# Two attention layers, a routed and a spline feed-forward on one core: causal row maxima taken with the mask added in the vector engine's own operation

## Chip, cores and metric

One NeuronCore of a Trainium2 chip runs the whole program. The metric is device time in microseconds (us), the median over several executions. Engines: TensorE (PE), VectorE (DVE), ScalarE (ACT), GpSimd (POOL), and SyncE (SP), which here only starts transfers (DMAs).

## The reference, cut to what matters

The input is x of shape 32 x 256 x 128 (32 sequences of 256 tokens, 128 features). Four blocks follow each other, each with a residual and a layer norm: attention with LoRA, a routed feed-forward of 8 experts, causal attention with rotary embedding, and a spline feed-forward. The change concerns the third:

```
qkv = x @ w_qkv                                  # 16 heads of 8 features
q, k = q * cos + rotate_half(q) * sin, k * cos + rotate_half(k) * sin
att = einsum('bhtd,bhsd->bhts', q, k) * scale
att = where(causal, att, finfo.min)
att = softmax(att, axis=-1)
y = einsum('bhts,bhsd->bhtd', att, v) ... @ w_proj
```

## The kernel before, in words

`attention` builds both attention layers: `attn0` (not causal) and `attn1` (causal, with rotary embedding). It is a software pipeline over the 32 sequences (`pipeline`, line 79): in each step every engine works on up to five sequences at different ages ("lag" 0 to 4), and each engine's program is written out by hand as 16 slots n = 0 to 15. The table `AT` says at which slot each small operation stands. Semaphores order the engines; a wait stops everything behind it on its engine.

A step of `attn1` does the following.

- Lag 0: PE transposes x (slot 0) and projects q and k (slot 1, L479); ACT copies them out of PSUM; POOL turns them (L257 to L261) and splits them into three bf16 parts (L267 to L277). SP stores the parts in a scratch in DRAM (L204, L206) and reads them back as the stacks `q_st` and `k_st` in six DMAs (L223). The six wait for the stores and, because they write the stack of three sequences ago, for that sequence's last column scores, which PE makes in slot 15 of the same step (`cols_ready`).
- Lag 2, the row scores, which serve only to find each query's maximum. `score_rows(st, n)` makes one unit per slot: unit u covers two heads and the query block t = u % 2, with (t + 1) * 128 keys per head, in one of three PSUM banks. Before it writes a bank it waits until DVE has taken the maximum of unit u - 3 (`max_kept`). In the causal layer it first writes the mask with one matmul (L531, 128 x 256: the identity times `mask_qk`, for both heads at once, over the diagonal blocks), and the two heads' products (L535) are added to it. `row_max` on DVE (L353) then reduces both heads in one instruction to two negated maxima in `negmax`. `split_max` (slot 9 for units 0 to 7, slot 15 for units 8 to 15) splits eight heads' maxima in two bf16 parts (L364, L366). PE transposes them (L471; slot 11 of this step, slot 1 of the next), ACT copies them, and SP places them as two more rows under q (L211, L195).
- Lag 3, the column scores: `score_cols(st, n)`, one head per slot, with the maximum already subtracted through those two rows and its own mask matmul (L553, L557); ACT takes the exponential (L297). Slot 0 waits for the first eight heads' maxima to land, slot 8 for the others (L195's DMA). `sum_values` (L574) multiplies by v in groups of four heads.
- Lag 4: transposing the output, dividing (DVE, L388 and L392, slot 3, after PE's L491 in slot 4), projection, residual, layer norm. v is copied by DVE at slot 5 (L381), the residual at slot 12 (L405, L409), the variance at slot 14 (L415, L418).

In each slot PE issues, in this order, the column scores, the row scores, and then whatever the table puts there; it has one queue. SP's queue in a step is: load of the next x (L186), L195, the two stores, L211, the six stack loads. DVE's slot begins with `row_max`.

`apart(eng, mem)` only adds one to a semaphore that nobody waits for; it keeps two waits from being merged. `mask_qk` is made once, before the first layer, by POOL in `prepare`. Masked places hold -1e30.

Of the kernel before, what the change touches and what calls it, by code (L numbers as in the profile page):

```python
# [9 lines left out]
BF16 = mybir.dt.bfloat16  # L10
I32 = mybir.dt.int32
ALU = mybir.AluOpType
ACT = mybir.ActivationFunctionType
AX_X = mybir.AxisListType.X

P = 128
B, N, C = 32, 256, 128
# [6 lines left out]
MASKED = -1e30  # L24
# [45 lines left out]
def apart(eng, mem):  # L70

    eng.sem_inc(mem["apart"], 1)


def wait(eng, sem, value):

    if not isinstance(value, int) or value > 0:
        eng.wait_ge(sem, value)
# [16 lines left out]
def attention(nc, name, mem, causal, x_dram, lora, rope):  # L95
# [7 lines left out]
    ident, ident_h, mask_qk, mask_kq = (mem[k] for k in ("ident", "ident_h", "mask_qk", "mask_kq"))  # L103
    scale = float(D) ** -0.5
# [3 lines left out]
    with ExitStack() as ctx:  # L108
        def sb(label, shape, dt=F32):
            return ctx.enter_context(nc.sbuf_tensor(f"{name}_{label}", shape, dt))  # L110

        def sem(label):
            return nc.alloc_semaphore(name=f"{name}_{label}")
# [8 lines left out]
        q_st = sb("q_st", [P, SLOTS, H, N], BF16)  # L122
        k_st = sb("k_st", [P, SLOTS, H, N], BF16)
        negmax = sb("negmax", [P, TB, H])
        mparts = sb("mparts", [P, 2, TB, MROWS, NH], BF16)
        mT_sb = sb("mT_sb", [MROWS * NH, 2, N], BF16)
        v_sb = sb("v_sb", [P, SLOTS, TB, H * 32])
# [12 lines left out]
        row_ps = ctx.enter_context(nc.psum_tensor(f"{name}_row_ps", [P, 3, 512], F32))  # L140
# [17 lines left out]
        xT_kept, qk_kept, v_kept, max_kept, mhi_kept, mparts_kept, mT_kept, probs_kept, oT_kept = (  # L158
            sem(x) for x in ("xT_kept", "qk_kept", "v_kept", "max_kept", "mhi_kept", "mparts_kept", "mT_kept",
                             "probs_kept", "oT_kept"))  # L160
# [13 lines left out]
        UNITS, ROW_BANKS = NH * TB, 3  # L174

        def row_bank(st, u):
            return (UNITS * st.off + u) % ROW_BANKS
# [166 lines left out]
        def _(dve):  # L344
            def row_max(st, u):

                p, t = u // TB, u % TB
                if u % NH == 0:

                    wait(dve, mparts_kept, st.seq(2, 2, u // NH - 1))  # L350
                dve.wait_ge(rows_ready, st.seq(2, UNITS, u + 1))
                keys = (t + 1) * P if causal else N
                nc.vector.tensor_reduce(  # L353
                    negmax[:, t, 2 * p:2 * p + 2],
                    row_ps[:, row_bank(st, u), 0:2 * keys].rearrange("p (a k) -> p a k", a=2),
                    AX_X, ALU.max, negate=True).then_inc(max_kept, 1)

            def split_max(st, g):

# [89 lines left out]
        def _(pe):  # L449
# [68 lines left out]
            def score_rows(st, u):  # L518

                sl = st.slot(2)  # L520
                p, t = u // TB, u % TB
                if u == 0:
                    pe.wait_ge(q_stacked[sl], st.turn(2, 16 * STACKS))
                    pe.wait_ge(k_stacked[sl], st.turn(2, 16 * STACKS))

                wait(pe, max_kept, st.seq(2, UNITS, u + 1 - ROW_BANKS))
                bank = row_ps[:, row_bank(st, u), :]
                keys = (t + 1) * P if causal else N
                if causal:
                    seen = bank[:, 0:2 * keys].rearrange("p (a k) -> p a k", a=2)  # L530
                    nc.tensor.matmul(seen[:, :, keys - P:keys], ident_h[:, :], mask_qk[:, :, :],  # L531
                                     start=True, stop=False, skip_group_check=True)
                for a in range(2):
                    h = 2 * p + a
                    last = nc.tensor.matmul(bank[:, a * keys:(a + 1) * keys],  # L535
                                            q_st[0:KROWS, sl, h, t * P:(t + 1) * P], k_st[0:KROWS, sl, h, 0:keys],
                                            start=not causal, stop=True, skip_group_check=causal)
                last.then_inc(rows_ready, 1)

            def score_cols(st, n):  # L540
# [1064 lines left out]
def prepare(nc, mem, w):  # L1605

    with ExitStack() as ctx:
# [3 lines left out]
        def sem(label):  # L1611
            return nc.alloc_semaphore(name=f"prep_{label}")
# [17 lines left out]
        loaded, consts, zeroed, masked = sem("loaded"), sem("consts"), sem("zeroed"), sem("masked")  # L1630
# [28 lines left out]
        @block.gpsimd  # L1659
        def _(pool):  # L1660
            for t in (mem["ident"], mem["ident_h"], mem["mask_qk"], mem["mask_kq"]):
                nc.gpsimd.memset(t[:], 0.0).then_inc(zeroed, 1)
            nc.gpsimd.memset(diagonal[:, :], 1.0).then_inc(zeroed, 1)
            nc.gpsimd.memset(mem["sigs"][:, :], 0.0).then_inc(zeroed, 1)
            nc.gpsimd.memset(mem["cw2"][:, :], 0.0).then_inc(zeroed, 1)
            nc.gpsimd.memset(mem["minus_half"][:, :], -0.5).then_inc(consts, 1)
            pool.wait_ge(zeroed, 7)
            for t in (mem["ident"], mem["ident_h"]):
                nc.gpsimd.affine_select(out=t[:, :], in_=t[:, :], compare_op=ALU.not_equal, fill=1.0, base=0,
                                        pattern=[[-1, P]], channel_multiplier=1).then_inc(consts, 1)  # L1670

            nc.gpsimd.affine_select(out=mem["mask_qk"][:], in_=mem["mask_qk"][:], compare_op=ALU.is_ge, fill=MASKED,
                                    base=0, pattern=[[0, 2], [-1, P]], channel_multiplier=1).then_inc(consts, 1)

            nc.gpsimd.affine_select(out=mem["mask_kq"][:], in_=mem["mask_kq"][:], compare_op=ALU.is_ge, fill=MASKED,
                                    base=0, pattern=[[0, 2], [1, P]], channel_multiplier=-1).then_inc(consts, 1)
            nc.gpsimd.affine_select(out=diagonal[:, :], in_=diagonal[:, :], compare_op=ALU.is_ge, fill=0.0,
                                    base=0, pattern=[[-D, H], [0, D]], channel_multiplier=1).then_inc(masked, 1)
            pool.wait_ge(masked, 1)
            nc.gpsimd.affine_select(out=diagonal[:, :], in_=diagonal[:, :], compare_op=ALU.is_ge, fill=0.0,  # L1680
                                    base=D - 1, pattern=[[D, H], [0, D]], channel_multiplier=-1).then_inc(consts, 1)
# [68 lines left out]
def build(nc, w, out):  # L1750
    with ExitStack() as ctx:
        def sb(label, shape, dt=F32):
            return ctx.enter_context(nc.sbuf_tensor(label, shape, dt))

        mem = {"x_all": sb("x_all", [P, TILES, C]), "x_mid": sb("x_mid", [P, TILES, C]),
               "ident": sb("ident", [P, P]), "ident_h": sb("ident_h", [P, P], BF16),
               "mask_qk": sb("mask_qk", [P, 2, P], BF16), "mask_kq": sb("mask_kq", [P, 2, P], BF16),
               "cos": sb("cos", [P, N]), "sin": sb("sin", [P, N]),
               "minus_half": sb("minus_half", [P, TILES])}
        for n in range(2):  # L1760
# [60 lines left out]
```

## Time and profile before

| what | us |
|---|---|
| median of 3 runs | 1542.13 |
| lowest and highest run | 1540.18, 1552.94 |
| the profiled execution, its own time | 1533.47 |
| its span in the profile | 1531.7 |

How to read it: the span begins with the first and ends with the last instruction that the profiler recorded. Busy time is the time in which an engine executes something; the matmuls' ends are modelled, so a busy PE is not PE at its peak. "PEld" is the loading of weights, which runs beside matmuls. "PEclk" is the granted clock of TensorE as a share of 2.4 GHz. Layer `attn0` runs from about 90 to 600 us of the span, `attn1` from about 700 to 1270 us.

### The profile page before, as it was taken

The numbers are of one execution on the slowest core, as the hardware profiler recorded it, in microseconds if no ns is written. First come the engines' busy times: TensorE is split into PE (matmuls) and PEld (weight loads), VectorE is DVE, ScalarE is ACT, GpSimd is POOL, SyncE is SP. The second block draws the span as 40 slices with busy tenths as digits, with TensorE's granted clock in tenths as the row PEclk, the third lists the DMA queues.
The fourth block names the chain that finished last, engine by engine and source line by source line (L and its number), as shares of the span: only waits on it lengthen the run. The fifth ranks groups of instructions, "written<-read, shape, count | busy, mean of one in ns | idle before, by whom it ended". The sixth has DMA issues, their size and how long they took to land. (4 is left out here: it accounts for less than half of the span.)

```text
span 1531.7 us, 36081 instructions
## 1 busy us (share of the span) xinstructions
PE 1142.7 (75%) x11411; PEld 786.7 (51%) x11411; DVE 1102.7 (72%) x2949; ACT 845.0 (55%) x1844; POOL 552.9 (36%) x572
## 2 busy tenths in 40 slices
PE   2699998999999987415999999999999984402220
PEld 1355655655565654203677767777777752202220
DVE  1477888888888886723677677767777757798996
ACT  1265666666666665442666666666666653302555
POOL 5222332223222311354444454445445305002555
PEclk9998999999999999756999999999999997755555
DMA  5644544445444540305444444454445302000011
GB/s 139 155 103 98 117 110 111 97 114 112 113 97 113 113 94 2 118 17 135 98 109 113 115 101 108 114 113 99 111 113 114 94 2 76 35 0 0 29 34 48
DMA packets 115921, 137.26 MB, mean 90 GB/s; under 512 B 12112, under 2 KB 101520, under 8 KB 106640
## 3 DMA queue, kind: packets, MB, share of 16 engines
q1 hardware_dynamic: 112704, 132.25, 36.2%
q10 hardware_dynamic: 3152, 4.20, 1.0%
q8 instruction: 34, 0.56, 0.2%
q14 instruction: 31, 0.25, 0.1%
HBM read 85.03 MB, written 37.75 MB: 80 GB/s over the span
## 5 line engine op out<-in xcount | busy, mean ns | idle before, releaser
L353 DVE TENSOR_REDUCE attn_negmax<-attn_row_ps 128x2 f32<-128x512 f32 (+1 forms) x1024 | 609.7, 618 | 283.0 <-PE attn_row_ps L535 273.7
L297 ACT ACTIVATE attn_probs<-attn_col_ps 128x512 f32<-128x512 f32 (+1 forms) x1024 | 542.5, 547 | 299.3 <-PE attn_col_ps L557 282.2
L557 PE MATMUL attn_col_ps<-attn_q_st,attn_k_st 74*128 74x256 bf16 (+1 forms) x2048 | 373.2, 264 | 36.7 <-DMA attn_q_st<-attn_mT_sb 34.6
L535 PE MATMUL attn_row_ps<-attn_k_st,attn_q_st 72*128 72x256 bf16 (+1 forms) x2048 | 375.3, 266 | 16.1 <-DMA attn_k_st<-attn_scratch 15.2
L574 PE MATMUL attn_out_ps<-attn_probs,attn_v_sb 128*32 128x256 f32 (+1 forms) x4096 | 255.1, 368 | 1.3 <-ACT attn_probs L297 1.3
L557 PEld LDWEIGHTS attn_col_ps<-attn_q_st,attn_k_st 74*128 74x128 bf16 x2048 | 180.6, 99 | 131.8 <-ACT attn_probs L297 41.0
L535 PEld LDWEIGHTS attn_row_ps<-attn_k_st,attn_q_st 72*128 72x128 bf16 x2048 | 204.4, 100 | 44.3 <-issue 16.7
L282 POOL TENSOR_TENSOR attn_rstd<-attn_var,minus_half 128x2 f32<-128x2 f32 x64 | 45.4, 710 | 459.7 <-DVE attn_var L418 459.7
L531 PE MATMUL attn_row_ps<-mask_qk,ident_h 128*128 128x256 bf16 x512 | 141.9, 277 | 23.5 <-DMA attn_k_st<-attn_scratch 23.5
L553 PE MATMUL attn_col_ps<-mask_kq,ident_h 128*128 128x256 bf16 x512 | 142.0, 277 | 23.3 <-DMA attn_q_st<-attn_mT_sb 22.1
L574 PEld LDWEIGHTS attn_out_ps<-attn_probs,attn_v_sb 128*32 128x32 f32 x4096 | 108.9, 111 | 90.0 <-issue 25.0
L257 POOL TENSOR_TENSOR attn_q_half<-attn_q_half,sin 128x512 f32<-128x512 f32 x32 | 40.7, 1272 | 146.4 <-ACT attn_qk L324 146.2
L1524 POOL TENSOR_TENSOR ffn_rstd<-ffn_var,minus_half 128x8 f32<-128x8 f32 x19 | 31.9, 1679 | 167.3 <-DVE ffn_var L1546 167.3
L479 PE MATMUL attn_in_ps<-attn_xT,wqk 128*128 128x256 f32 x256 | 80.6, 442 | 1.8 <-ACT attn_xT L303 1.8
L553 PEld LDWEIGHTS attn_col_ps<-mask_kq,ident_h 128*128 128x128 bf16 x512 | 49.9, 97 | 61.7 <-DMA attn_q_st<-attn_mT_sb 25.1
L267 POOL TENSOR_SCALAR attn_parts<-attn_qk 128x512 bf16<-128x512 f32 x64 | 39.5, 618 | 113.6 <-ACT attn_qk L321 102.1
L1468 PE MATMUL ffn_r_ps<-ffn_table_hm,ffn_ohT 128*128 128x193 bf16 x64 | 21.0, 361 | 75.0 <-ACT ffn_ohT L1480 75.0
L277 POOL TENSOR_TENSOR attn_parts<-attn_rest,attn_parts 128x512 bf16<-128x512 f32 x64 | 74.3, 1162 | 5.4
L270 POOL TENSOR_TENSOR attn_rest<-attn_qk,attn_parts 128x512 f32<-128x512 f32 x64 | 74.0, 1156 | 5.4
L531 PEld LDWEIGHTS attn_row_ps<-mask_qk,ident_h 128*128 128x128 bf16 x512 | 49.6, 97 | 33.0 <-issue 24.2
L1457 PE MATMUL ffn_o_ps<-ident_h,ffn_onehot 128*128 128x128 bf16 x64 | 10.1, 313 | 73.4 <-PEq L1172 73.4
L1487 ACT ACTIVATE ffn_z<-ffn_y,ffn_shift,ffn_rstd 128x128 f32<-128x128 f32 x64 | 26.3, 482 | 55.5 <-DVE ffn_shift L1551 55.5
(229 smaller groups left out, 1694.5 us busy)
## 6 DMA issues: line engine op xcount, KB each, us to landing
attn_q_st<-attn_scratch SPq DMA_DIRECT2D x192, 192.0 KB
attn_k_st<-attn_scratch SPq DMA_DIRECT2D x192, 192.0 KB
attn_scratch<-attn_parts SPq DMA_DIRECT2D x64, 384.0 KB, 2.8
attn_scratch<-attn_parts SPq DMA_DIRECT2D x64, 128.0 KB, 2.8
attn_x_in<-in_L_attn_x_dram SPq DMA_DIRECT2D x32, 128.0 KB, 7.0
moe_xs<-x_all SPq DMA_DIRECT2D x8, 512.0 KB, 3.1
attn_x_in<-x_mid SPq DMA_DIRECT2D x32, 128.0 KB, 7.0
ffn_xs<-x_mid SPq DMA_DIRECT2D x16, 256.0 KB, 2.3
```

The source lines that it names most:

```text
L257: nc.gpsimd.tensor_tensor(q_half[:, :, :], q_half[:, :, :], sin, ALU.mult).then_inc(sin_done, 1)
L270: nc.gpsimd.tensor_tensor(rest[:, :, :], qk[:, :, :], parts[:, :, 0, :], ALU.subtract)\
L277: nc.gpsimd.tensor_tensor(parts[:, :, 2, :], rest[:, :, :], parts[:, :, 1, :], ALU.subtract)\
L282: nc.gpsimd.tensor_tensor(rstd[:, :], var[:, :], mem["minus_half"][:, 0:TB], ALU.pow)\
L297: nc.scalar.activation(probs[:, u % 2, j, 0:W], col_ps[:, n % 2, 0:W], ACT.Exp, scale=scale).then_inc(probs_kept, 1)
L353: nc.vector.tensor_reduce(negmax[:, t, 2 * p:2 * p + 2], row_ps[:, row_bank(st, u), 0:2 * keys].rearrange("p (a k) -> p a k", a=2), AX_X, ...
L479: last = nc.tensor.matmul(in_ps[:, s * N:(s + 1) * N], wqk[:, s, :], xT[:, st.slot(0), :], start=True, stop=True)
L531: nc.tensor.matmul(seen[:, :, keys - P:keys], ident_h[:, :], mask_qk[:, :, :], start=True, stop=False, skip_group_check=True)
L535: last = nc.tensor.matmul(bank[:, a * keys:(a + 1) * keys], q_st[0:KROWS, sl, h, t * P:(t + 1) * P], k_st[0:KROWS, sl, h, 0:keys], start=n ...
L553: nc.tensor.matmul(seen[:, :, 0:P], ident_h[:, :], mask_kq[:, :, :], start=True, stop=False, skip_group_check=True)
L557: last = nc.tensor.matmul(bank[:, t * N:(t + 1) * N - first], k_st[0:rows, sl, h, t * P:(t + 1) * P], q_st[0:rows, sl, h, first:N], start= ...
L574: last = nc.tensor.matmul(out_ps[32 * j:32 * j + 32, g * N + first:(g + 1) * N], v_sb[:, st.slot(lag), t, 32 * h:32 * h + 32], probs[:, u ...
```

## The change

For the causal layer the mask matmul under the row scores is left out, so that the two head products start their own accumulation. On DVE the one reduction over two heads becomes two `tensor_tensor_reduce` operations, one per head. Each reads the head's scores from PSUM and the mask from SBUF (fp32, 256 columns: zeros over the first 128 keys, the triangle over the last 128; a unit with 128 keys reads the last 128), adds them, multiplies by -1, writes the sum as bf16 to a buffer `unread` that nobody reads, and gives the minimum as the negated maximum. `unread` has two halves, so a unit waits until the unit two before it has finished. The first layer keeps its reduction.

```diff
+        unread = sb("unread", [P, 2, 2, N], BF16) if causal else None
...
                 dve.wait_ge(rows_ready, st.seq(2, UNITS, u + 1))
-                keys = (t + 1) * P if causal else N
-                nc.vector.tensor_reduce(
-                    negmax[:, t, 2 * p:2 * p + 2],
-                    row_ps[:, row_bank(st, u), 0:2 * keys].rearrange("p (a k) -> p a k", a=2),
-                    AX_X, ALU.max, negate=True).then_inc(max_kept, 1)
+                if not causal:
+                    nc.vector.tensor_reduce(
...
+                    return
+                apart(dve, mem)
+                wait(dve, max_kept, st.seq(2, UNITS, u - 1))
+                apart(dve, mem)
+                keys = (t + 1) * P
+                for a in range(2):
+                    last = nc.vector.tensor_tensor_reduce(
+                        out=unread[:, u % 2, a, 0:keys], in0=row_ps[:, row_bank(st, u), a * keys:(a + 1) * keys],
+                        in1=mask_qk[:, N - keys:N], scale=-1.0, scalar=3e38, op0=ALU.add, op1=ALU.min,
+                        accum_out=negmax[:, t, 2 * p + a:2 * p + a + 1])
+                last.then_inc(max_kept, 1)
...
                 keys = (t + 1) * P if causal else N
-                if causal:
-                    seen = bank[:, 0:2 * keys].rearrange("p (a k) -> p a k", a=2)
-                    nc.tensor.matmul(seen[:, :, keys - P:keys], ident_h[:, :], mask_qk[:, :, :],
-                                     start=True, stop=False, skip_group_check=True)
                 for a in range(2):
                     h = 2 * p + a
                     last = nc.tensor.matmul(bank[:, a * keys:(a + 1) * keys],
                                             q_st[0:KROWS, sl, h, t * P:(t + 1) * P], k_st[0:KROWS, sl, h, 0:keys],
-                                            start=not causal, stop=True, skip_group_check=causal)
+                                            start=True, stop=True)
...
-            nc.gpsimd.affine_select(out=mem["mask_qk"][:], in_=mem["mask_qk"][:], compare_op=ALU.is_ge, fill=MASKED,
-                                    base=0, pattern=[[0, 2], [-1, P]], channel_multiplier=1).then_inc(consts, 1)
+            nc.gpsimd.affine_select(out=mem["mask_qk"][:, P:N], in_=mem["mask_qk"][:, P:N], compare_op=ALU.is_ge,
+                                    fill=MASKED, base=0, pattern=[[-1, P]], channel_multiplier=1).then_inc(consts, 1)
...
-               "mask_qk": sb("mask_qk", [P, 2, P], BF16), "mask_kq": sb("mask_kq", [P, 2, P], BF16),
+               "mask_qk": sb("mask_qk", [P, N]), "mask_kq": sb("mask_kq", [P, 2, P], BF16),
```

## Rows read from the trace of the kernel before

**Rows 1.** The page, busy time of each engine over the whole span
```profile
PE 1142.7 (75%) x11411; PEld 786.7 (51%) x11411; DVE 1102.7 (72%) x2949; ACT 845.0 (55%) x1844; POOL 552.9 (36%) x572
```
**Rows 2.** Windows (length, busy time per engine, PEclk, DMA): causal layer; two steps of the first
```profile
751.50:1270.00 518.50, 487.89 (x5505) 361.89 (x5503) 367.18 (x998) 324.97 (x739) 225.18 (x235) 0.99 0.43 101
388.20:404.40 16.20, 15.11 (x154) 9.98 (x152) 14.03 (x34) 11.17 (x24) 4.96 (x6) 1.00 0.49 114
404.40:422.30 17.90, 16.33 (x152) 10.40 (x151) 13.88 (x34) 11.23 (x25) 4.95 (x6) 0.91 0.45 103
```
**Rows 3.** Timeline (start us, duration us), ACT's copy L338, which comes once per step
```profile
852.82 0.36 ACT L338 COPY attn_mT_sb<-attn_in_ps 16x256 bf16<-16x256 bf16 x1
1175.47 0.36 ACT L338 COPY attn_mT_sb<-attn_in_ps 16x256 bf16<-16x256 bf16 x1
...
388.22 0.34 ACT L338 COPY attn_mT_sb<-attn_in_ps 16x256 bf16<-16x256 bf16 x1
404.43 0.34 ACT L338 COPY attn_mT_sb<-attn_in_ps 16x256 bf16<-16x256 bf16 x1
422.29 0.34 ACT L338 COPY attn_mT_sb<-attn_in_ps 16x256 bf16<-16x256 bf16 x1
```
**Rows 4.** Timeline of PE in one step of the causal layer
```profile
1036.02 0.28 PE L553 MATMUL attn_col_ps<-mask_kq,ident_h 128*128 128x256 bf16 x1 [0.71 <-DMA attn_q_st<-attn_mT_sb]
...
1043.01 0.27 PE L531 MATMUL attn_row_ps<-mask_qk,ident_h 128*128 128x256 bf16 x1
1043.12 0.38 PE L535 MATMUL attn_row_ps<-attn_k_st,attn_q_st 72*128 72x256 bf16 x2
...
1044.80 0.27 PE L471 MATMUL attn_fin_ps<-ident_h,attn_mparts 128*16 128x128 bf16 x2
```
**Rows 5.** Timeline of SP's queue in the same step
```profile
1043.20 0.32 SPq L223 DMA_DIRECT2D attn_q_st<-attn_scratch  x1
...
1046.41 0.63 SPq L195 DMA_DIRECT2D attn_q_st<-attn_mT_sb  x1
```
**Rows 6.** Waits of SP's queue, 860 to 1160 us (us in total, times, longest)
```profile
SPq L72 <- DMA attn_scratch<-attn_parts: 25.2, 18, 1.5
SPq L223 <- PE attn_col_ps L557: 4.8, 11, 0.9
```
**Rows 7.** Waits, 751.5 to 1270 us (us in total, times, longest)
```profile
DVE attn_negmax L353 <- PE attn_row_ps L535: 91.6, 159, 1.3
...
PEld attn_in_ps L501 <- ACT attn_qk L324: 6.6, 27, 0.3
```
**Rows 8.** Groups by shape, 760 to 1240 us (busy us, mean ns | idle before)
```profile
L353 DVE TENSOR_REDUCE attn_negmax<-attn_row_ps 128x2 f32<-128x512 f32 x228 | 156.4, 686 | 60.0 <-PE attn_row_ps L535 57.4
L353 DVE TENSOR_REDUCE attn_negmax<-attn_row_ps 128x2 f32<-128x256 f32 x228 | 95.4, 418 | 35.2 <-PE attn_row_ps L535 31.3
...
L392 DVE TENSOR_TENSOR attn_o_sb<-attn_fin_ps,attn_rden 128x128 f32<-128x128 f32 x58 | 14.1, 285 | 1.0
L405 DVE TENSOR_TENSOR attn_y_sb<-attn_fin_ps,x_mid 128x256 f32<-128x256 f32 x28 | 11.9, 424 | 5.0 <-PE attn_fin_ps L514 4.7
L415 DVE BATCH_NORM_AGGREGATE attn_mv<-attn_stats 128x2 f32<-128x6 f32 x56 | 6.6, 159 | 0.0
```
**Rows 9.** Timeline of DVE in one step of the causal layer
```profile
1032.73 0.36 DVE L388 RECIPROCAL attn_rden<-attn_fin_ps 128x32 f32<-128x32 f32 x1 [0.90 <-PE attn_fin_ps L491]
1033.12 0.49 DVE L392 TENSOR_TENSOR attn_o_sb<-attn_fin_ps,attn_rden 128x128 f32<-128x128 f32 x2
...
1042.83 0.23 DVE L415 BATCH_NORM_AGGREGATE attn_mv<-attn_stats 128x2 f32<-128x6 f32 x2
...
1044.47 0.17 DVE L366 TENSOR_TENSOR attn_mparts<-attn_negmax,attn_mparts 128x16 bf16<-128x16 f32 x1
...
1049.77 0.36 DVE L388 RECIPROCAL attn_rden<-attn_fin_ps 128x32 f32<-128x32 f32 x1 [0.91 <-PE attn_fin_ps L491]
```
**Rows 10.** Windows: DVE's stretch in that step, all engines, then L353 alone
```profile
1032.73:1044.64 11.91, 11.20 (x136) 8.36 (x134) 10.09 (x28) 6.71 (x15) 6.43 (x7) 1.00 0.33 84
...
1032.73:1044.64 11.91, 6.46 (x12) 1.00 0.33 84
```
**Rows 11.** Line L405, 860 to 1160 us: DVE's sequencer computing a wait's value (ns, min/median/max)
```profile
L405 DVEq FUSED_REGOPS  x18: 57/65/81, 870.9 to 1159.5; - x18
```

More of the change, by code:

```diff
@@ L351, in row_max @@
                 dve.wait_ge(rows_ready, st.seq(2, UNITS, u + 1))
-                keys = (t + 1) * P if causal else N
-                nc.vector.tensor_reduce(
-                    negmax[:, t, 2 * p:2 * p + 2],
-                    row_ps[:, row_bank(st, u), 0:2 * keys].rearrange("p (a k) -> p a k", a=2),
-                    AX_X, ALU.max, negate=True).then_inc(max_kept, 1)
+                if not causal:
+                    nc.vector.tensor_reduce(
+                        negmax[:, t, 2 * p:2 * p + 2],
+                        row_ps[:, row_bank(st, u), :].rearrange("p (a k) -> p a k", a=2),
+                        AX_X, ALU.max, negate=True).then_inc(max_kept, 1)
+                    return
[9 more added lines that the diff above has]
+                last.then_inc(max_kept, 1)
             def split_max(st, g):
```

## The prediction

> **What bounds the kernel now.** I read the page's busy line first: PE 75% and DVE 72% of the span, neither alone the bound [rows 1]. The windows view then isolates the causal layer, the only one whose steps the change touches: in 518.5 us PE is busy 487.9 us (94%), DVE 367.2 us (71%), at a granted clock of 0.99 [rows 2]. So TensorE looks like the bound and VectorE as if it had room. The step view corrects this. Nineteen steps lie between the two marks of ACT's copy, (1175.47 - 852.82) / 19 = 16.98 us each [rows 3]. In one of them PE stands still for 0.71 us at slot 8, waiting for the second half of the maxima to land from DMA [rows 4]. A full engine would not wait, so I followed that wait back through SP's timeline: the small DMA L195 is issued at 1046.41, behind the six stack loads that start at 1043.20 [rows 5], and the stack loads are released by PE's last column scores (slot 15; its row scores follow at 1043.12 [rows 4]) or by the stores before them. Both come nearly together: SP waited 25.2 us in 18 steps for the stores, and after that 4.8 us for PE [rows 6], 0.27 us a step.
>
> That gives three closed chains, and the longest sets the step:
> - Chain A: PE slot 8 (1036.02) to the stack loads (1043.20), 7.18 us, then the DMAs until the next slot 8, 16.98 - 7.18 = 9.8 us. Its length is the step itself.
> - Chain B: the same, but through q and k, ACT, POOL and the stores; it runs over two steps and is at most 0.27 us behind.
> - Chain C: DVE's second split ends (1044.47 + 0.17 = 1044.64 [rows 9]), PE transposes it at 1044.80 [rows 4], PE works through slots 1 to 4, DVE starts L388 at 1049.77 [rows 9], and then does twelve units and its other work until the next second split ends. Now it has slack: in the stretch from L388 (1032.73) to 1044.64 DVE is busy 10.09 of 11.91 us [rows 10]. Its length is 0.16 + 4.97 + 10.1 + about 0.3 of gaps between dependent instructions (of the 1.8 us idle the timeline puts most on PE; 0.3 is my estimate for the rest) = 15.5 us, 1.5 under the step.
>
> **The change, part by part.** *PE.* It loses 16 mask matmuls a step. One takes 1043.12 - 1043.01 = 0.11 us of PE's time [rows 4] (their 0.27 us are mostly pipeline), 1.8 us a step; over 32 steps that is 57 us of TensorE work gone. But chain A holds only the seven between slot 8 and slot 15's column scores: 7 x 0.115 = 0.8 us, so A becomes 16.2 us. Chain B sees the saving once in two steps: (2 x 17.0 - 0.27 - 0.92 - 0.2) / 2 = 16.3 us, and 16.4 with a later split. In chain C two of the three masks lie in front of PE's projection of v, which waits for ACT anyway (27 times, up to 0.3 us [rows 7]): only one counts, 4.97 becomes 4.85. *If nothing else changed*, the step would be 16.4 us, 0.6 less.
>
> *DVE.* The reduction over 512 elements takes 686 ns and over 256 elements 418 ns [rows 8]; twelve of them keep DVE busy 6.46 us, 0.54 a unit [rows 10]. In their place come two operations per unit of 256 or of 128 elements, each with PSUM and SBUF inputs. The trace has both shapes as plain additions: L405 (256) 424 ns and L392 (128) 285 ns [rows 8], so the slope is 139 / 128 = 1.09 ns per element and the rest some 145 ns. Back to back less counts: two L392 take 0.49 us together [rows 9], so the second starts 0.205 us after the first, which is 0.133 for its elements at the reductions' slope ((686 - 418) / 256 = 1.05 ns) and 0.07 fixed. Two heads then cost 2 x (0.267 + 0.07) = 0.68 us at 256 and 2 x (0.134 + 0.07) = 0.41 us at 128, mean 0.54: no more than today's 0.54.
>
> What no row shows is a DVE operation that gives a stream and a reduced value both. Bound from below: nothing, 0.54 a unit. Below nothing is excluded, since the same elements pass at the same slope. Bound from above: each head runs to its full end (424 or 285 ns) and then a small instruction with its full 159 ns (L415 [rows 8]) writes the value: (2 x 0.583 + 2 x 0.444) / 2 = 1.03 us a unit. I take a small instruction that is pipelined like the others: two L415 take 0.23 us [rows 9], 0.07 more than one. That is 0.14 a unit, 0.68 us in all. I take it because the reduced value can only be known after the last element, and L415 is the nearest row for a result of so few elements.
>
> The Trainium skill, "VectorE: DVE Perf Modes", section "Two Vector instructions with no wait between them", says that an operation that also writes out its accumulator is two instructions, the main one and an accumulator read. No row here shows one; by that rule the unit would be at the 0.68 and not at the 0.54, and it speaks against the change.
>
> Chain C then: 0.16 + 4.85 + other DVE work 10.09 - 6.46 = 3.63 + 12 x 0.68 = 8.2 + 0.3 = 17.1 us. This is now the longest chain, by 0.7 us over B: the idle time of DVE (91.6 us of waits for row scores [rows 7]) is used up, and PE waits for the second split in slot 1. PE's waits in slot 1 and DVE's three-bank lead do not help, since the split needs all eight pairs.
>
> *The added wait and markers.* The wait is for the unit two before, which has finished when the one before runs; behind it stand this unit's operations and all later DVE work. Value 0 as long as the sequencer runs ahead. Computing a wait's value takes 65 ns (57 to 81) of DVE's sequencer [rows 11]; if that and two markers were exposed, it is up to 3 x 0.065 = 0.2 us a unit. I take 0, with that as the upper end. *One-time parts* (the mask made once, fp32 in place of bf16; no DMA is added or moved): 0, before the first layer and behind its loads. The first layer is unchanged. The stack loads keep their place in SP's queue, and when C rules they start later.
>
> *The clock.* The first layer has no mask matmuls, and its steps show what may follow: one of 16.2 us at granted clock 1.00 is followed by one of 17.9 us at 0.91 [rows 2, 3]; at two levels (2.4 and 1.2 GHz) that is some 18% of the step at the lower one. The steps are 404.43 - 388.22 = 16.21 and 422.29 - 404.43 = 17.86 us, so a fall costs up to 1.65 us, and they come in about one step of three, 0.55 us a step. The causal layer, fuller, is at 0.99. After the change PE has 1.8 us less work and slightly longer steps, like the first layer. Since PE is no longer in the longest chain for most of the step, I take half, 0.27 us.
>
> The page "TensorE: Matmul & The Clock Gate" of the Trainium skill, section "Part 1: The HAM clock gate (the "warmup" mystery)", says that the slow clock is the default and activity releases it; by it, taking matmuls out can bring the slow clock back, as the first layer's row of 0.91 suggests.
>
> **Sum.** 17.1 + 0.27 - 16.98 = 0.39 us a step, 31 full steps: +12 us. The profiled execution took 1533.5 us, so 1545.5 us on its basis. The median of the runs, 1542.1 us, lies 8.6 us above that execution; I add the difference to the median: 1554 us. A change under 1% (15.4 us) can't be told from none here.
>
> **Rivals.**
> - R1, the reduced value comes free. Unit 0.54 us, chain C 15.5 us, the step is 16.4 from chain B: -0.58 x 31 = -18 us, 1524; with falls of the clock as above -10 us, 1532. For it: the plain additions' rows. Against: nothing shows two results at the price of one.
> - R2, the value is read only after the operation has drained. Unit up to 1.03, chain C 0.16 + 4.85 + 3.63 + 12.4 + 0.3 = 21.3 us: +4.3 x 31 = +134 us, 1676. It decides from a unit above 0.66 us, where C passes today's 16.98. For it: dependent instructions on DVE do show their full latency (L366 starts 0.2 us after the cast before it). Half of it (0.85) gives C 19.1 and +67 us, 1609.
> - R3, the sequencer is exposed (0.2 us a unit over the forecast): unit 0.88, chain C 19.5, +2.5 x 31 = +78 us at full price, 1620, and 1595 at two thirds. For it: a unit now has a second wait, two markers and two dispatches. Against: where DVE is behind, it has a unit's time to do them.
> - R4, the clock falls in every step, 1.4 to 1.6 us each, with cheap maxima: 16.4 + 1.5 = 17.9, +28 us, 1570. Against: in the first layer it falls in one of three.
>
> **Chances.** Forecast 0.42, R1 0.20, R2 0.13, R3 0.15, R4 0.10. Within the forecast's own spread (unit 0.62 to 0.75, clock 0 to 0.5 us) somewhat under half lies above +15.4 us. Faster by over 1%: half of R1 and a little of the forecast, 0.13. Within 1%: the rest of R1 and over half of the forecast, 0.37. Slower: 0.50. The range leaves out R1's last part and R2's upper half: 1524 to 1609.
>
> **What would show it.** Right: DVE's waits for row scores in the causal layer fall from 91.6 us to under 30; the two operations of a 256-key unit span some 0.8 us; PE waits for `attn_mparts` at slot 1 in most steps; the wait at slot 8 for L195 stays or shrinks; PE busy falls by about 50 us; steps of 17.1 to 17.6 us; PEclk of the layer 0.95 to 0.98. Wrong: if DVE still waits often for row scores and steps are under 16.6 us, the value came free (R1). If a head's operation and its end take over 0.5 us at 256, it is R2; if the operations are short but stand apart by 0.1 us or more with nothing released between them, R3; if the clock is under 0.93 with cheap operations, R4.

## The result and the profile after

The changed kernel takes 1578.5 us (median of 4 runs, 1572.1 to 1582.6) against 1541.2 us before: a ratio of 1.022, 95% interval 1.016 to 1.029. It is slower by 37 us. The profiled execution took 1580.4 us. The chip shows a faster and a slower state at the same kernel: ratios here compare executions in the faster one, times are medians of all.

The page's busy line and the windows view of the causal layer (columns as in [rows 2]) for the changed kernel:

```profile
PE 1121.6 (71%) x10899; PEld 751.5 (48%) x10899; DVE 1142.5 (72%) x4485; ACT 844.4 (53%) x1844; POOL 553.4 (35%) x572
```
```profile
751.50:1270.00 518.50, 437.73 (x4637) 309.59 (x4639) 372.55 (x2239) 301.16 (x688) 217.66 (x217) 0.93 0.43 99
```

TensorE lost 512 matmuls, as written, but only 21 us of busy time in the whole span, where the prediction had 57: its granted clock in this layer went from 0.99 [rows 2] to 0.93, and what is left runs longer. VectorE's busy time in the window, 372.6 us against 367.2 [rows 2], can't be compared as it stands, because fewer steps fit into the window now. In the whole span it is 40 us more (1142.5 against 1102.7 [rows 1]), and the row maxima alone, in a window of their own, before and then after, are:

```profile
860.00:1150.00 290.00, 146.58 (x274) 1.00 0.47 110
```
```profile
860.00:1150.00 290.00, 149.38 (x968) 0.93 0.43 100
```

That is 146.58 / 274 = 0.53 us a unit before and, with four instructions to a unit, 149.38 / 242 = 0.62 us after: 0.08 more, 1.3 us a step. The marks of ACT's copy, one per step (start, duration; L339 answers to L338 [rows 3]), show where the time is:

```profile
878.16 0.36 ACT L339 COPY attn_mT_sb<-attn_in_ps 16x256 bf16<-16x256 bf16 x1
...
894.53 0.36 ACT L339 COPY attn_mT_sb<-attn_in_ps 16x256 bf16<-16x256 bf16 x1
...
911.91 0.36 ACT L339 COPY attn_mT_sb<-attn_in_ps 16x256 bf16<-16x256 bf16 x1
...
937.29 0.36 ACT L339 COPY attn_mT_sb<-attn_in_ps 16x256 bf16<-16x256 bf16 x1
```

The steps are 16.4, 17.4 and 25.4 us, and so it goes on: one step in three takes 20 to 25 us. The others take 16.3 to 18.7 us, the shortest as long as the prediction had it for cheap maxima. The waits view of the same layer (us in total, times, longest) names the place:

```profile
DVE attn_unread L364 <- issue: 60.3, 50, 8.4
DVE attn_unread L364 <- PE attn_row_ps L543: 49.7, 77, 2.1
...
PEld attn_row_ps L543 <- DVE attn_negmax L364: 35.1, 9, 6.8
PE attn_row_ps L543 <- DVE attn_negmax L364: 33.0, 7, 6.6
```

"issue" is time in which the engine waited for nothing that the profile shows. VectorE stands still for 60.3 us without a releaser, up to 8.4 us at once, and TensorE then waits for it up to 6.6 us; before, this wait was 0.2 us, once. VectorE's timeline at one of these places:

```profile
804.35 0.60 DVE L435 TENSOR_SCALAR x_mid<-attn_y_sb,attn_mv,attn_rstd 128x128 f32 x2
813.38 0.29 DVE L364 CUSTOM_DVE_ANT_0 attn_unread<-attn_row_ps,mask_qk 128x128 bf16<-128x128 f32 x1 [8.44 <-issue]
```

L435 is the last operation of slot 15, and the next is slot 0 of the next step. The loop of `pipeline` covers three steps and makes eight turns, so it jumps back seven times, after a slot 15. Seven stalls (they end at 813.4, 868.6, 925.7, 984.7, 1039.7, 1096.0 and 1151.5 us) come in this place, 55 to 59 us apart, once per turn, 46 us together. An eighth, of 4.2 us, ends at 1232.6 us, in the steps that are written out behind the loop. The view of DMA queues, window 820 to 1190 us (packets, MB, share of the 16 engines; queue q14 is the one that grows here), of the kernel before and then of the changed one:

```profile
q8 instruction: 2, 0.03, 0.0%
q14 instruction: 1, 0.01, 0.0%
```
```profile
q14 instruction: 32, 0.26, 0.3%
```

Before, no engine needed more than stray packets of code in the middle of the loop. Now 32 packets of 8 KB are fetched, about five per turn. Counted in the built programs, VectorE's loop body in the causal layer has 432 instructions; before it had 190. That is the theory tested below, F: the body no longer stays in the engine's instruction memory, and each jump back waits for code. (TensorE's body in the same layer had 540 instructions before and has 492 now, and before the change hardly a packet in the middle of the loop went with it: the length that matters is not the same for both engines.)

The packets can be set beside the stalls one by one. The stall that ends at 868.60 us begins at 862.49. Between 861 and 865 us no instruction packet starts; the queues from 865 to 867 us are:

```profile
q1 hardware_dynamic: 90, 0.32, 75.6%
q14 instruction: 1, 0.01, 2.0%
```

In all 21 stalls at a jump, of this kernel and of experiments 2 and 4, the packet records have one instruction packet inside, and VectorE goes on 2.1 to 2.4 us after it ends. What differs is when it starts: 1.1 to 5.7 us after VectorE has stopped. In 20 of them the burst of the six stack loads had begun before the stall and 12 to 14 packets of data were on their way at once. In the one where the burst began 0.6 us after the stall, the packet started after 1.1 us, and this stall is the shortest, 3.8 us. So most of a long stall looks like a code packet that waits among the loads; no run moved the loads to test it.

The new operations themselves are cheap. Groups by shape, 760 to 1270 us, and VectorE's timeline inside a full stretch:

```profile
L364 DVE CUSTOM_DVE_ANT_0 attn_unread<-attn_row_ps,mask_qk 128x256 bf16<-128x256 f32 x437 | 167.5, 421 | 39.2 <-PE attn_row_ps L543 31.8 <-DVE attn_negmax L364 2.6 <-issue 2.4
...
L364 DVE CUSTOM_DVE_ANT_0 attn_unread<-attn_row_ps,mask_qk 128x128 bf16<-128x128 f32 x436 | 108.7, 287 | 76.8 <-issue 57.9 <-PE attn_row_ps L543 16.4 <-DVE attn_negmax L364 1.7
...
L364 DVE DVE_READ_ACCUMULATOR2_ANT attn_negmax<- 128x1 f32 x872 | 72.3, 83 | 0.0
```
```profile
1061.14 0.42 DVE L364 CUSTOM_DVE_ANT_0 attn_unread<-attn_row_ps,mask_qk 128x256 bf16<-128x256 f32 x1
1061.49 0.08 DVE L364 DVE_READ_ACCUMULATOR2_ANT attn_negmax<- 128x1 f32 x1
1061.49 0.42 DVE L364 CUSTOM_DVE_ANT_0 attn_unread<-attn_row_ps,mask_qk 128x256 bf16<-128x256 f32 x1
1061.83 0.08 DVE L364 DVE_READ_ACCUMULATOR2_ANT attn_negmax<- 128x1 f32 x1
1061.83 0.49 DVE L393 COPY attn_v_sb<-attn_in_ps 128x128 f32<-128x128 f32 x2
```

421 and 287 ns are the plain additions' 424 and 285 [rows 8]. The accumulator read is there as an instruction of its own, of 83 ns, but the next operation starts together with it: from one head to the next it is 0.34 us, the prediction's 0.267 + 0.07 without anything for the read.

### The profile page after: what moved, and what is told of

Its sections match the earlier page's. It is cut to its first block and busy times, and to the rows that moved or that the text cites. A ratio compares the mean times of both kernels' runs of the same rounds, so it can differ in the third digit from the quotient of the medians.

```text
span 1578.7 us, 37619 instructions
## 1 busy us (share of the span) xinstructions
PE 1121.6 (71%) x10899; PEld 751.5 (48%) x10899; DVE 1142.5 (72%) x4485; ACT 844.4 (53%) x1844; POOL 553.4 (35%) x572
## 5 line engine op out<-in xcount | busy, mean ns | idle before, releaser
L364 DVE CUSTOM_DVE_ANT_0 attn_unread<-attn_row_ps,mask_qk 128x128 bf16<-128x128 f32 (+1 forms) x1024 | 313.3, 354 | 178.1 <-PE attn_row_ps L543 108.8
L543 PE MATMUL attn_row_ps<-attn_k_st,attn_q_st 72*128 72x256 bf16 (+1 forms) x2048 | 382.2, 270 | 73.4 <-DMA attn_k_st<-attn_scratch 38.4
L354 DVE TENSOR_REDUCE attn_negmax<-attn_row_ps 128x2 f32<-128x512 f32 x512 | 335.2, 684 | 122.2 <-PE attn_row_ps L543 120.0
L565 PE MATMUL attn_col_ps<-attn_q_st,attn_k_st 74*128 74x256 bf16 (+1 forms) x2048 | 380.1, 268 | 37.9 <-DMA attn_q_st<-attn_mT_sb 35.7
L582 PE MATMUL attn_out_ps<-attn_probs,attn_v_sb 128*32 128x256 f32 (+1 forms) x4096 | 258.6, 372 | 1.3 <-ACT attn_probs L298 1.3
L565 PEld LDWEIGHTS attn_col_ps<-attn_q_st,attn_k_st 74*128 74x128 bf16 x2048 | 184.4, 101 | 136.9 <-ACT attn_probs L298 41.2
L543 PEld LDWEIGHTS attn_row_ps<-attn_k_st,attn_q_st 72*128 72x128 bf16 x2048 | 184.7, 101 | 109.1 <-issue 40.8
L561 PE MATMUL attn_col_ps<-mask_kq,ident_h 128*128 128x256 bf16 x512 | 148.3, 290 | 38.3 <-DMA attn_q_st<-attn_mT_sb 36.7
L364 DVE DVE_READ_ACCUMULATOR2_ANT attn_negmax<- 128x1 f32 x1024 | 85.0, 83 | 0.0
```

What stands on the lines that cost most here:

```text
L354: nc.vector.tensor_reduce(negmax[:, t, 2 * p:2 * p + 2], row_ps[:, row_bank(st, u), :].rearrange("p (a k) -> p a k", a=2), AX_X, ALU.max, ...
L364: last = nc.vector.tensor_tensor_reduce(out=unread[:, u % 2, a, 0:keys], in0=row_ps[:, row_bank(st, u), a * keys:(a + 1) * keys], in1=mask ...
L543: last = nc.tensor.matmul(bank[:, a * keys:(a + 1) * keys], q_st[0:KROWS, sl, h, t * P:(t + 1) * P], k_st[0:KROWS, sl, h, 0:keys], start=T ...
L561: nc.tensor.matmul(seen[:, :, 0:P], ident_h[:, :], mask_kq[:, :, :], start=True, stop=False, skip_group_check=True)
L565: last = nc.tensor.matmul(bank[:, t * N:(t + 1) * N - first], k_st[0:rows, sl, h, t * P:(t + 1) * P], q_st[0:rows, sl, h, first:N], start= ...
L582: last = nc.tensor.matmul(out_ps[32 * j:32 * j + 32, g * N + first:(g + 1) * N], v_sb[:, st.slot(lag), t, 32 * h:32 * h + 32], probs[:, u ...
```

## The experiments

Ratios are against runs of the kernel before on the same chip. Its median there was 1541.6 us for experiments 1, 2, 3 and 6, 1541.4 us for 4, 7, 8 and 10, and 1538.5 us for 5, 9, 11 and 12. Where two experiments ran on different chips, their ratios are compared and not their times. "Steps without a fall" are those between two marks of ACT's copy, from 830 to 1185 us, in which the granted clock stays at 1.00.

**1. The loop written out.**

```diff
-            pipeline(dve, step)
+            if causal:
+                for s in range(B + DEPTH - 1):
+                    step(Step(0, s, SLOTS, B))
+            else:
+                pipeline(dve, step)
```

> The changed kernel with one difference: in the causal layer VectorE's program is written out for all sequences instead of looping three steps at a time; the same operations in the same order, no jump back. Theory F (VectorE's loop body, now 432 instructions against 190 before, no longer stays in its instruction memory, and each jump back waits for code to be fetched): the idle times of 4 to 8 us once per three steps vanish, steps are 16.3 to 16.8 us throughout, the time is about 1520 to 1535 us, below the kernel before. Rival O (the new operations themselves, or the reading of their accumulator, now and then hang back for microseconds): the same 4 to 8 us stalls stay, about 1578 us. Rival C (TensorE's clock falls and costs the time): about 1570 us, granted clock as low as in the changed kernel.

Measured 1547.2 us, ratio 1.003 (0.999 to 1.006). Windows view and VectorE's wait for row scores in the waits view, causal layer:

```profile
751.50:1270.00 518.50, 458.36 (x5036) 320.46 (x5034) 399.74 (x2385) 323.00 (x739) 219.74 (x220) 0.97 0.44 100
```
```profile
DVE attn_unread L364 <- PE attn_row_ps L547: 54.6, 75, 2.1
```

The long stalls are gone, the longest wait without a releaser is 1.9 us, and with them go 31 us (the ratio falls from 1.022 to 1.003). Rival O falls: the same 1024 operations are there. What is left of the loss is within the noise, but the expected gain (1520 to 1535 us) didn't come either. The steps without a fall take 16.9 us, 17 of them, and 4 steps of 21 have a fall of the clock. Code is still fetched, in the same window of the queues:

```profile
q14 instruction: 19, 0.16, 0.2%
```

Nineteen packets, about one per step, and VectorE doesn't stop for them. So the packets alone are not the cost; the wait for one at a jump back is.

**2 and 3. Old operations, long loop; and the same without a loop.** Five markers per unit bring the old kernel's body to 430 instructions:

```diff
                 dve.wait_ge(rows_ready, st.seq(2, UNITS, u + 1))
+                if causal:
+                    for _ in range(5):
+                        apart(dve, mem)
```

> The kernel before, with five idle markers (additions to a semaphore nobody waits for) ahead of each row maximum in the causal layer, so that VectorE's loop body has 430 instructions, as many as in the changed kernel, but all of the old operations. Theory F: one stall of 4 to 8 us per three steps appears, 7 to 9 of them, and the time rises by 30 to 60 us, to 1570 to 1600 us. Rival O: no such stalls, 1540 to 1550 us.

> As the run with five markers, but with VectorE's causal program written out without a loop. It prices the markers alone. Theory F: no long stalls, 1540 to 1550 us, so that what the run with the loop has more is the jump back. Rival M (the markers take sequencer time and this is the cost): the same time as with the loop.

Measured 1592.5 us with the loop (ratio 1.034, 1.029 to 1.040) and 1561.4 us without (1.013, 1.007 to 1.019). The timeline and the DMA queues (820 to 1190 us) of the one with the loop show the same picture with `tensor_reduce`:

```profile
868.32 0.60 DVE L426 TENSOR_SCALAR x_mid<-attn_y_sb,attn_mv,attn_rstd 128x128 f32 x2
874.59 0.42 DVE L356 TENSOR_REDUCE attn_negmax<-attn_row_ps 128x2 f32<-128x256 f32 x1 [5.67 <-issue]
```
```profile
q14 instruction: 33, 0.27, 0.2%
```

33 packets against the changed kernel's 32, and the loop costs 1592.5 - 1561.4 = 31 us, the same as in the changed kernel. The markers themselves cost 20 us, more than the 10 at most that I had expected: steps of 17.4 us against 16.98. They stand between TensorE's signal and each reduction, so they aren't hidden where VectorE waits. (Two markers, experiment 5, cost nearly nothing: the price doesn't grow evenly with their number.) Theory F was put to a kernel with nothing new but length, and held.

**4 and 5. How long is too long.** The changed kernel with one marker and no wait (382 instructions, loop kept), and the kernel before with two markers (286):

```diff
                 apart(dve, mem)
-                wait(dve, max_kept, st.seq(2, UNITS, u - 1))
-                apart(dve, mem)
...
-                        out=unread[:, u % 2, a, 0:keys], ...
+                        out=unread[:, u, a, 0:keys], ...
```

> The changed kernel with its loop, but one marker per unit instead of a wait and two markers (16 places for the unread sums): VectorE's loop body has 382 instructions instead of 432. Theory F with a limit between 382 and 432: stalls vanish, about 1545 us. Theory F with the limit below 382: stalls of 4 to 8 us stay, once in three steps, about 1575 us. Rival S (the added wait causes the stalls): they vanish whatever the length.

> The kernel before with two idle markers per unit in place of five: VectorE's loop body in the causal layer has 286 instructions (190 before, 382 and 430 to 432 stall). Theory F with its limit above 286: no stalls, 1545 to 1552 us. With the limit below 286: a stall of 4 to 8 us once in three steps, 1570 to 1585 us.

With 382 instructions 1572.3 us (ratio 1.018, 1.012 to 1.023), seven stalls of 5.8 to 6.7 us: too long still, and the added wait is cleared of it (rival S). With 286 instructions 1539.7 us (1.002, 0.998 to 1.005), below the 1545 us at least that I had expected; no stall, and the queues between 820 and 1190 us as before the change:

```profile
q8 instruction: 2, 0.03, 0.0%
q14 instruction: 1, 0.01, 0.0%
```

The limit for this loop lies between 286 and 382. The Trainium skill, "Runtime: NRT & Kernel Launch", section "Instruction fetch mechanics", gives most engines an instruction memory of 32 KiB, 512 instructions, filled in blocks of 256, and says that a taken branch whose target is outside the two blocks held forces a fetch. By two whole blocks one would expect 382 to fit when it is well placed; these runs show a limit below that, which a body that begins inside a block would give. They don't show where the blocks begin, so this reading of the limit isn't tested; that a jump outside what is held waits for a fetch agrees with the packets inside the stalls.

**6. TensorE's part alone.** The mask matmul is dropped and the old reduction kept; the row maxima then leave the causal mask out.

```diff
-                if causal:
-                    seen = bank[:, 0:2 * keys].rearrange("p (a k) -> p a k", a=2)
-                    nc.tensor.matmul(seen[:, :, keys - P:keys], ident_h[:, :], mask_qk[:, :, :],
-                                     start=True, stop=False, skip_group_check=True)
...
-                                            start=not causal, stop=True, skip_group_check=causal)
+                                            start=True, stop=True)
```

> The kernel before without the mask matmul under the row scores, the old single reduction kept: the row maxima then leave the causal mask out. It is the PE part of the change alone. Chain view of the prediction: the step falls to 16.4 us at best, -18 us, or -10 us if the clock falls as in the first layer: 1523 to 1532 us. Rival (PE was the bound with all of its 1.8 us a step): 1490 us.

Measured 1546.0 us, ratio 1.002 (0.996 to 1.007): neither. Taking matmuls away that the prediction put at 57 us changed nothing. Windows view, and the marks of ACT's copy:

```profile
751.50:1270.00 518.50, 463.43 (x5010) 323.29 (x5010) 352.29 (x980) 321.62 (x736) 219.62 (x220) 0.95 0.43 99
```
```profile
851.01 0.36 ACT L338 COPY attn_mT_sb<-attn_in_ps 16x256 bf16<-16x256 bf16 x1
...
867.41 0.36 ACT L338 COPY attn_mT_sb<-attn_in_ps 16x256 bf16<-16x256 bf16 x1
...
885.64 0.36 ACT L338 COPY attn_mT_sb<-attn_in_ps 16x256 bf16<-16x256 bf16 x1 [0.32 <-PE attn_in_ps L471]
```

A step without a fall of the clock is 867.41 - 851.01 = 16.4 us, the length that chain B gave. The next is 18.2 us. The granted clock over the layer is 0.95 where it was 0.99, and 11 of 21 steps are of the long kind, 18.2 us in the mean. This became theory K: the freed time of TensorE lets its clock fall, and the fall takes the gain back.

**7 to 9. TensorE's idle time filled.** Six matmuls into a bank that the following scores overwrite, ahead of slot 8, in the lean written-out version (control: the same without them), and in the kernel of experiment 6:

```diff
+            def fill(st, u):
+                wait(pe, max_kept, st.seq(2, UNITS, u + 1 - ROW_BANKS))
+                for _ in range(6):
+                    nc.tensor.matmul(row_ps[:, row_bank(st, u), 0:N], ident_h[:, :],
+                                     mask_kq[:, :, :].rearrange("p a k -> p (a k)"), start=True, stop=True)
...
                 for n in range(H):
+                    if causal and n == 8 and st.has(2):
+                        fill(st, n)
                     if st.has(3):
                         score_cols(st, n)
```

> The changed kernel with VectorE's causal program written out without a loop, and without the added wait and its two markers per unit (the unread sums get 16 places instead of 2). Against the run that is only written out (1547 us): theory S (the wait and markers hold VectorE's sequencer up in places, the 0.2 us gaps ahead of some units) expects 3 to 10 us less, 1537 to 1544 us; theory 0 (they are hidden) the same 1547 us.

> The lean written-out version plus six matmuls per step whose result is overwritten, placed on TensorE just ahead of slot 8, where it waits for the maxima to land anyway (0.66 us of TensorE's time a step). Theory K (the clock of TensorE falls because it has too little to do, and that gives the saved matmuls' time back): the granted clock in the causal layer returns to 0.99, the steps with a fall (18 to 20 us) vanish, all are 16.3 to 16.8 us, 1520 to 1530 us. Rival W (the falls are not TensorE's doing but come from the waits, so extra work only adds time): clock stays at 0.95 to 0.97 and the time rises by up to 0.66 x 31 = 20 us.

> The kernel before without the mask matmul under the row scores (the row maxima leave the causal mask out), the old single reduction and the loop kept, plus six matmuls with an overwritten result ahead of slot 8. It repeats the test of the clock with nothing new on VectorE. Theory K: against the same kernel without the six (1546 us) the falls of the clock vanish, steps 16.3 to 16.8 us, 1525 to 1532 us. Rival (the clock's gain in the other pair was chance): 1540 us or more.

Without the six 1545.2 us (ratio 1.000, 0.997 to 1.003). With them 1532.9 us (0.992, 0.988 to 0.995), 12 us less on the same chip. In the kernel of experiment 6 the ratio falls from 1.002 (0.996 to 1.007) to 0.989 (0.985 to 0.993), some 19 us, give or take 10; the time is 1524.1 us. Windows of the two that are filled, lean version first, and TensorE's timeline at slot 8 of the lean one:

```profile
751.50:1270.00 518.50, 473.04 (x5259) 335.18 (x5255) 401.97 (x2421) 325.12 (x746) 228.14 (x238) 0.98 0.44 101
```
```profile
751.50:1270.00 518.50, 469.82 (x5219) 334.15 (x5217) 369.03 (x1004) 322.26 (x740) 231.83 (x240) 0.98 0.44 101
```
```profile
1139.64 0.82 PE L593 MATMUL attn_row_ps<-mask_kq,ident_h 128*128 128x256 bf16 x6
1141.27 0.28 PE L562 MATMUL attn_col_ps<-mask_kq,ident_h 128*128 128x256 bf16 x1 [0.81 <-DMA attn_q_st<-attn_mT_sb]
```

Work whose result nobody uses makes both kernels faster, by 12 and some 19 us: it lies in a wait (0.81 us of it are even left) and the clock is granted at 0.98. Steps with a fall go from 7 to 2 and from 11 to none, of 21 each, and the steps without one stay as they were (16.6 us in the lean version, 16.5 and 16.6 us in the other). Theory K held in both pairs, though the clock stops short of the 0.99 that I expected; rival W falls. The Trainium skill, "TensorE: Matmul & The Clock Gate", section "Part 1: The HAM clock gate (the "warmup" mystery)", has the slow clock as the default and activity as what releases it; these pairs agree.

What the added wait and its markers cost (theory S) is not settled by the times: experiment 7 is some 4 us below experiment 1 by the ratios, give or take 8. The waits views of the causal layer are clearer. With them (experiment 1) and then without (experiment 8):

```profile
PE attn_fin_ps L487 <- DVE attn_mparts L378: 11.9, 21, 1.0
DVE attn_unread L364 <- DVE attn_negmax L364: 11.4, 24, 0.9
DVE attn_unread L364 <- issue: 10.2, 11, 1.9
```
```profile
PE attn_fin_ps L484 <- DVE attn_mparts L375: 3.7, 12, 0.6
DVE attn_unread L361 <- issue: 0.2, 1, 0.2
```

With the wait and markers VectorE stands 22 us for itself and its sequencer, TensorE waits longer for the split, and the steps without a fall take 16.9 us in place of 16.6: 0.3 us a step, some 9 us in all. The time shows only half of it, since the longer steps come with fewer falls of the clock (4 of 21 in experiment 1, 7 of 21 in experiment 7). So theory S held in part. The new operations themselves make a step at most 0.1 us longer (16.64 us in experiment 8 against 16.57 in experiment 9).

**10. TensorE's work put back.** The written-out changed kernel with one overwritten matmul of the old mask's shape ahead of every unit.

```diff
+                if causal:
+                    nc.tensor.matmul(bank[:, 0:N], ident_h[:, :], mask_kq[:, :, :].rearrange("p a k -> p (a k)"),
+                                     start=True, stop=True)
                 for a in range(2):
```

> The written-out changed kernel with a matmul of the old mask's shape put back ahead of every unit's row scores (its result is overwritten), so TensorE's work is that of the kernel before while VectorE has the new operations. Theory K: granted clock 0.99 in the causal layer, steps of 17.0 us throughout, 1540 to 1548 us, no faster and no slower than without these matmuls. Rival D (VectorE's new operations are in the longest chain): steps over 17.3 us, 1552 us or more.

Measured 1548.4 us, ratio 1.004 (1.001 to 1.008), clock 0.99:

```profile
751.50:1270.00 518.50, 488.73 (x5468) 361.14 (x5467) 403.50 (x2396) 323.54 (x734) 221.95 (x222) 0.99 0.44 100
```

Sixteen matmuls more or less per step give the same ratio within the noise (1.004 and 1.003). It is also the measure of VectorE's part, operations, wait and markers together, with TensorE's work as before: 0.4%, some 7 us. That lies between the two expectations: the upper end of the interval, 1553 us, touches rival D's 1552, and the 20 steps without a fall take 17.3 us in the mean, where I expected 17.0 and D wants over 17.3. VectorE's part is not free.

**11 and 12. The first layer too.** `if n == 8 and st.has(2)` in the lean version, and `if not causal and ...` in the otherwise untouched kernel before.

> The lean written-out version with the six overwritten matmuls ahead of slot 8 in both attention layers. The first layer has 24 us at the lower clock in the kernel before, and its steps with a fall are 1.65 us longer, about nine of them. Theory K: they vanish, 10 to 15 us less than with the causal layer's six alone (1533 us), 1518 to 1524 us. Rival: in the first layer VectorE and TensorE are so full that 0.66 us of work is not hidden, no gain, 1530 to 1540 us.

> The kernel before with the six overwritten matmuls ahead of slot 8 in the first layer only, the causal layer untouched. Theory K: the first layer's falls vanish, 10 to 15 us less than before, 1527 to 1532 us. Rival as in the run with both: no gain, 1540 us.

1517.0 us (ratio 0.985, 0.981 to 0.989) and 1525.5 us (0.990, 0.985 to 0.994). Windows of the first layer, of the kernel before and then of the one with the fill there alone:

```profile
200.00:600.00 400.00, 365.38 (x3582) 236.26 (x3584) 329.08 (x777) 263.75 (x541) 108.36 (x132) 0.97 0.44 100
```
```profile
200.00:600.00 400.00, 373.55 (x3750) 246.46 (x3748) 330.63 (x786) 265.74 (x544) 110.12 (x135) 1.00 0.44 100
```

The falls of [rows 2] are gone (1.00), and the first layer gives 13 us that have nothing to do with the change. The version with both is the fastest of all: 21 us under the kernel before and, by the ratios, some 58 us under the changed one.

## Why the prediction came out as it did

It forecast 1554 us, slower at a chance of one half, in 1524 to 1609; measured 1578.5. The direction and the range held, but by luck: 31 of the 37 us come from a cost that stands in no term and in no rival. Without it (experiment 1) the kernel is at 1.003 (0.999 to 1.006), where the forecast had 12 us more than before.

- *What bounds the kernel; chains A and B.* Right. Steps of 16.4 us, chain B's length, appear wherever neither the clock nor code nor VectorE's wait is in the way (experiment 6).
- *PE loses 1.8 us a step, and only part of it counts.* Right. With the clock kept up (experiment 9) TensorE's part brings a ratio of 0.989, 17 us, against the 18 us of R1. Without that it brings nothing (1.002).
- *The price of the reduced value: twice too high.* I took 0.07 us per head for the read, 0.14 a unit, to get 0.68. The read exists and lasts 83 ns, but the next operation starts together with it: start to start a unit takes (2 x 0.34 + 2 x 0.21) / 2 = 0.55 us. That must not be set beside the 0.54 of before, as the working did: 0.54 is busy time to the end of each reduction, and from start to start the old unit takes, by the working's own slope and 0.07 fixed, (0.61 + 0.34) / 2 = 0.475 us. In one measure for both, busy time, it is 0.62 against 0.53. So the unit costs 0.08 us more, halfway between R1 (nothing) and the forecast (0.14). Bounding the read by the distance of two L415 was the faulty step, since two instructions of one kind say nothing of how a read follows the operation it belongs to. The rule of the Trainium skill, that such an operation is two instructions, is borne out by the rows; the price was my addition.
- *Chain C.* With 0.62 it comes to 0.16 + 4.85 + 3.63 + 12 x 0.62 + 0.3 = 16.4 us, level with chain B and not 0.7 us above it. VectorE still waits 49.7 us for row scores, where I had written under 30. But the chain is not out of play either: TensorE waits for the second split, as forecast (11.9 us, 21 times in experiment 1), and with the wait and markers in it the steps without a fall are 16.9 us, near the forecast's 17.1.
- *The clock.* The mechanism was right, the size off by two or more. I took 0.27 us a step, 8 us in all; experiments 6 and 9 differ by some 19 us, the whole of TensorE's gain, and the falls come in 11 of 21 steps, not one in three. Halving the first layer's price because "PE is no longer in the longest chain" rested on chain C.
- *The sequencer (R3).* The value 0 for the added wait and markers was too low: some 0.3 us a step, about an eighth of what R3 had at full price. The instructions had another price that no part of the sum asked for: their number in a loop. It is 31 us, the largest term of all and 83% of the 37 us: 7 stalls of 5 to 8 us at the jump, not 512 small ones.

So the sum by what the runs showed, each taken from ratios and known to 6 to 10 us: -17 us for the shorter chain (experiment 9), +19 us for the clock (experiments 6 and 9), +31 us for the code (the changed kernel and experiment 1), and for VectorE's operations, wait and markers 2 us (experiments 1 and 6) to 7 us (experiment 10, with the clock at 0.99). That is 35 to 40 us; measured 37. What is left open: whether the stalls would shrink if the six stack loads, 1.2 MB on the same 16 DMA engines, came at another time; the packet records suggest it, no run tried it.

## What to carry to other kernels

Count the instructions of a hand-written loop body, markers and accumulator reads too, before and after a change: between 286 and 382 on VectorE a loop began to wait for code at each jump, and writing it out made the wait vanish, though not the packets. The sign is a stall without a releaser at the loop's first instruction, with a packet in an instruction queue inside it; packets alone are no sign. When TensorE's work is taken away while it waits for a DMA anyway, look first at its granted clock, in a layer that already has as little work too; here a few dead matmuls in the wait were worth as much as the matmuls saved. And compare two operations in one measure: from start to start, or as busy time, not one by each.

## What the hardware showed that I had not expected

- An accumulator read of 83 ns that starts with the next operation and costs nothing from start to start (0.34 us for 256 elements, 0.21 for 128).
- A loop of 382, 430 or 432 instructions on VectorE stalls 4 to 8 us per turn, one of 190 or 286 doesn't, whatever the operations in it.
- In each of the 21 stalls one 8 KB packet of code starts 1.1 to 5.7 us after the engine has stopped, and the engine goes on 2.1 to 2.4 us after the packet's end.
- Six dead matmuls in a step bring 12 and some 19 us in the causal layer and 13 in the first, at granted clocks of 0.98 and 1.00 in place of 0.95 to 0.97.
- Five markers per unit, on an engine that is idle a quarter of the time, cost 20 us, two cost 2 us or nothing: what stands between a signal and the operation that waits for it is not always covered by idle time.
